# Splitting a resident weight slot two places earlier, and giving one low half in seven to GpSimd

## The reference

```python
x = x + tanh(g_xattn) * xattn(layernorm(x), ctx, mask, Wq, Wk, Wv, Wo, q_norm, k_norm)   # x: 16 x 128 x 1024, 32 heads, 8 KV heads
x = x + tanh(g_ffn) * ffn(layernorm(x), A, B, Wr)
# ffn: scores = x @ Wr.T (64 experts), top 16, softmax -> gates G
#      h = einsum('nd,krd->nkr', x, A);  y = 2 * einsum('nkr,kdr->nd', h * G, B)
```

## Time and profile before

| | us |
|---|---|
| median of 3 executions | 2399.37 (2396.16 to 2401.35) |
| the profiled execution's own time | 2401.17 |
| its span on the core | 2399.4 |
| PE busy | 2289.7 (95%) |
| PEld busy | 1924.3 (80%) |
| DVE busy | 1614.7 (67%) |
| POOL busy | 1313.9 (55%) |
| ACT busy | 1179.2 (49%) |

### The profile page before, as it was taken

The page is one execution under the profiler, slowest core; times in us unless marked ns, Lnnn a source line. Parts: engine busy times, 40 slices in busy tenths (PEclk is TensorE's granted clock), DMA queues, the critical chain, the costliest instruction groups (busy, mean ns, idle before and its releaser), DMA issues.

```text
span 2399.4 us, 35662 instructions
## 1 busy us (share of the span) xinstructions
PE 2289.7 (95%) x11600; PEld 1924.3 (80%) x11600; DVE 1614.7 (67%) x2651; ACT 1179.2 (49%) x3763; POOL 1313.9 (55%) x1811
## 2 busy tenths in 40 slices
PE   5998998999999989999999699999899999999899
PEld 4886887888888878888888588788787787788687
DVE  6557457777777787777777745755756877644755
ACT  4455545666666676666666622422423334333421
POOL 5566567655555575555555344654645655343421
PEclk8999999999999999999999799999999999999999
DMA  4687546757767457742233444545546357324653
GB/s 169 217 229 271 179 158 235 207 165 203 191 167 210 126 175 194 196 135 88 90 95 114 146 159 158 210 167 173 195 159 245 129 204 264 113 81 131 231 174 132
DMA packets 180231, 412.98 MB, mean 172 GB/s; under 512 B 12176, under 2 KB 77968, under 8 KB 164624
## 3 DMA queue, kind: packets, MB, share of 16 engines
q1 hardware_dynamic: 176016, 381.34, 46.6%
q0 software_dynamic: 4032, 29.36, 6.9%
HBM read 293.21 MB, written 176.16 MB: 196 GB/s over the span
## 4 chain that ended last, share of the span: by engine, by line
PE 88%; DVE 3%; issue 3%; POOL 3%; DMA 2%; ACT 1%; SPq 0%; POOLq 0%; ACTq 0%; DVEq 0%
PE bank L706 24%; PE bank L708 24%; PE bank L707 24%; PE bank L764 4%; PE bank L772 2%; PE bank L752 2%; DVE t_lo L1226 1%; PE bank L787 1%; PE bank L789 1%; PE bank L788 1%; DVE s_lo L1226 1%; DMA staged<-in_w_q 1%; PE bank L740 1%; PE bank L723 1%; PE bank L804 1%
## 5 line engine op out<-in xcount | busy, mean ns | idle before, releaser
L706 PE MATMUL bank<-t_hi,s_hi 128*128 128x512 f32 x2688 | 1091.1, 406 | 74.8 <-issue 42.4
L708 PE MATMUL bank<-t_hi,s_lo 128*128 128x512 f32 x2688 | 1059.3, 394 | 0.0
L707 PE MATMUL bank<-t_lo,s_hi 128*128 128x512 f32 x2688 | 1056.9, 393 | 0.0
L706 PEld LDWEIGHTS bank<-t_hi,s_hi 128*128 128x128 f32 x2688 | 510.9, 190 | 182.5 <-issue 82.9
L1226 DVE TENSOR_TENSOR s_lo<-staged,s_hi 128x512 fp32r<-128x512 f32 x672 | 539.9, 848 | 98.9 <-ACT s_hi L954 91.3
L708 PEld LDWEIGHTS bank<-t_hi,s_lo 128*128 128x128 f32 x2688 | 509.3, 189 | 112.1
L707 PEld LDWEIGHTS bank<-t_lo,s_hi 128*128 128x128 f32 x2688 | 511.4, 190 | 91.4
L954 ACT CAST s_hi<-staged 128x512 fp32r<-128x512 f32 x448 | 258.3, 623 | 359.3 <-DMA staged<-heads 190.0
L1646 POOL TENSOR_SCALAR small<-small 128x4 f32<-128x4 f32 (+1 forms) x192 | 65.5, 341 | 417.7 <-ACT small L1039 338.0
L1661 POOL TENSOR_TENSOR staged<-staged 128x512 f32<-128x512 f32 x96 | 136.9, 1426 | 257.3 <-DMA staged<-gated 86.1
L1735 POOL TENSOR_TENSOR sums<-sums,usum 128x512 f32<-128x512 f32 x64 | 97.1, 1538 | 210.5 <-DVE usum L1240 188.7
(11 more groups left out here) (126 smaller groups left out, 2981.1 us busy)
## 6 DMA issues: line engine op xcount, KB each, us to landing
heads<-heads SPq DMA_DIRECT2D x128, 256.0 KB, 3.7
t_raw<-combos SPq DMA_DIRECT2D x28, 1024.0 KB, 8.5
t_raw<-in_sets SPq DMA_DIRECT2D x25, 1024.0 KB, 8.2
staged<-in_w_q SPq DMA_DIRECT2D x32, 768.0 KB, 5.7
staged<-heads SPq DMA_DIRECT2D x32, 768.0 KB, 5.8
sums<-sums SPq DMA_DIRECT2D x18, 1024.0 KB, 7.9
sums<-sums SPq DMA_DIRECT2D x36, 512.0 KB, 4.7
xt<-x_columns SPq DMA_DIRECT2D x8, 1792.0 KB, 7.3
```

The lines of the kernel that those rows point to most:

```text
L706: nc.tensor.matmul(out, s_hi[w][:, cols], high, start=start, stop=False, skip_group_check=True)
L707: nc.tensor.matmul(out, s_hi[w][:, cols], low, start=False, stop=False, skip_group_check=True)
L708: done = nc.tensor.matmul(out, s_lo[w][:, cols], high, start=False, stop=at == 3, skip_group_check=True)
```

## The change

It does four things. (1) The table for the turns at entries 8, 16, 58, 66, 74, 82 and 90 becomes (2, 3, 4, 5, 6, 7, 8): slots 0 to 3 are split two places earlier in the order of ACT and DVE, slots 4 to 6 three places earlier. The turns at 32 and 50 keep their table. (2) From the turn at entry 58 on (set number t of 5 and more), `t_lo[5]` is made by a subtraction on GpSimd instead of DVE; GpSimd has a `fill_t` for it at the end of each place. (3) SP issues the next entry's `staged` ahead of the refill of slot 1 instead of behind it (in the loops with keys and values, output projection and A; not in the query loop). (4) PE's wait on the low half counts on two semaphores instead of one.

```diff
-FILL_POSITIONS = (4, 5, 6, 7, 9, 10, 11)
+FILL_POSITIONS = (2, 3, 4, 5, 6, 7, 8)
...
+    def low_by_pool(self, t, k):
+
+        return t >= 5 and k == 5
+
+    def t_low(self, t, k):
+
+        if self.low_by_pool(t, k):
+            return t - 4
+        return self.t_fill(t, k) - max(t - 5, 0) - (1 if t >= 5 and self.t_order[t].index(k) > 5 else 0)
...
             for j in SEVEN:
-                refill(e, entries[e].ks[j])
                 if j == 1:
                     stage(e + 1, e)
+                refill(e, entries[e].ks[j])
...
-                refill(e, j)
...
                 if j == 1:
                     stage(e + 1, e)
-                    if q and sums_stored(q - 1):
-                        sums_out(q - 1)
+                refill(e, j)
+                if j == 1 and q and sums_stored(q - 1):
+                    sums_out(q - 1)
...
                 if plan.first_of_set[entry.tau] == e:
-                    pe.wait_ge(t_lo_done, plan.t_fill(entry.tau, k))
+                    pe.wait_ge(t_lo_pool if plan.low_by_pool(entry.tau, k) else t_lo_done, plan.t_low(entry.tau, k))
...
             for tau, k in plan.t_due.get(beat, ()):
+                if plan.low_by_pool(tau, k):
+                    continue
                 dve.wait_ge(t_hi_done, plan.t_fill(tau, k))
...
     def _(pool):
+        def fill_t(beat):
+            for tau, k in plan.t_due.get(beat, ()):
+                if plan.low_by_pool(tau, k):
+                    pool.wait_ge(t_hi_done, plan.t_fill(tau, k))
+                    nc.gpsimd.tensor_tensor(t_lo[k][:, :, :], t_raw[k][:, :, :], t_hi[k][:, :, :].bitcast(FP32),
+                                            ALU.subtract).then_inc(t_lo_pool, 1)
```

More of the change, by code:

```diff
@@ L306, in program @@
     t_hi_done, t_lo_done, t0_combo, t0_combo_pool = sem("t_hi_done"), sem("t_lo_done"), sem("t0_combo"), sem("t0_combo_pool")
+    t_lo_pool = sem("t_lo_pool")
     st_in, st12_in = sem("staged_in"), sem("staged12_in")
@@ L1809, in _ @@
                         router_weights()
+                fill_t(plan.beat0[e] + j)
         for e in range(A0, ENTRIES):
```

## The result

The changed kernel takes 2404.27 us (median of 20 executions, 2399.85 to 2411.74) against 2400.23 us (20 executions on the same chip). The ratio is 1.0022, 95% interval 1.0014 to 1.0029: slower by some 4 to 5 us. The forecast was 2392.5 us and 2377 to 2403: the sign was wrong and the time lies just outside the range. The profiled execution's span is 2406.9 us, 7.5 over that of before. That is more than the medians differ by: the profiled execution took 2408.69 us, 4.4 over the median of its kernel, and the one of before 2401.17, 0.9 over.

What follows compares the result with a forecast made beforehand. It took PE, busy 95% of the span, to be held at a turn by DVE's queue, which starts late. Terms 3 x 0 - 4.5 + 1 - 1.0 - 2.4 = -6.9 us gave 2394.3, as median 2392.5 us; range 2377 to 2403.

Steps and rivals of the forecast that it cites:

- The blocking of DVE: At turns with a GpSimd half, DVE stands until GpSimd's long subtraction is through: between 0 and 4.45 us, upper end taken.
- The -4.5 for the turn to 8: Turn to entry 8, no GpSimd half: starts later but ends at 232.9 against 237.43, a win of 4.5 us.
- the +1 for the turn to 16: Turn to entry 16: the phase's last transposes wait behind more resident slots, 1 us lost (from -2 to +4).
- the walk for entry 74: Step-by-step timing of the turn to entry 74: PE stands 4.6 us at the head, product 6 ends at 1879.5, before 1879.51.
- PE does products 0 to 3 without a wait from 1857.0 to 1867.8: In entry 74, behind the 4.6 us wait at its head, PE runs four products without waiting.
- Term: 0.0 us for each of the three turns of the output projection: Turns to entries 58, 66 and 74: slots 4 to 6 early, the evacuation late in their place, no net change.
- rival (b): ACT and DVE stand at a landing, one-piece head gap, clock falls: 2 us at each of six turns, 2407 us, chance 0.18.
- The terms for entries 82 and 90: Turns to entries 82 and 90: wins of 1.0 and 2.4 us, with `s_lo[6]` delayed at both.
- rival (a): The turns open fully, DVE not standing for GpSimd's long subtraction or standing idle: -25 us, time 2374, chance 0.25.
- Point (c): Nothing measurable: at every turn the gap moves from the entry's middle to its head and back; within 4 us of 2399, chance 0.17.
- 0.3 us on the landing of slot 2: Turn to entry 74: SP's new order lands slot 2 0.3 us later and brings `staged` 2.2 us earlier, unused.

Runs made afterwards that it cites:

- the four pieces: The changed kernel with GpSimd's 128x2048 subtraction issued as four of 128x512: 2394.26 us, ratio 0.9969 to the kernel before.
- the memset: The changed kernel with GpSimd's 128x2048 subtraction replaced by a memset of the same tile: 2393.17 us, ratio 0.9962 to the kernel before.
- the sixteen transposes: The changed kernel plus sixteen identity transposes on PE behind product 6 of entries 57, 65 and 73: 2402.22 us, ratio 1.0012 to the kernel before.
- the version that reaches it: The kernel before with table (2, 3, 5, 6, 7, 8, 9), SP's old order, no low half on GpSimd: 2373.42 us, ratio 0.9890.
- the places alone: The kernel before with only the new table (2, 3, 4, 5, 6, 7, 8): 2387.07 us, ratio 0.9953.
- Sixteen 128x128 transposes: The kernel with only the new table, plus identity transposes on PE behind product 6 of entries 57, 65, 73: 2383.04 us, ratio 0.9920 to the kernel before.

## Why the prediction was wrong

**What held.** The blocking of DVE was priced at 4.45 us and measured at 4.69 behind a subtraction of 4.62; the four pieces and the memset show that it is one long instruction that reads SBUF which holds it. This is what the Trainium skill, SBUF — State Buffer, "Who interferes with whom", states of a two-input DVE instruction against a reading GpSimd instruction; the trace agrees (4.69 us), and so does the `s_lo` beside the memset (0.69). The -4.5 for the turn to 8 came out at -4.5, and there the walk had 2.5 us for the slow clock behind the gap (entry 8 took 2.7 us over its 20.88). The same program took 51.3 to 53.8 us there in other executions, so the exact hit is luck. So is the +1 for the turn to 16, which came out at +1.4: the scatter between equal programs is 2.2 us there, and its mechanism was not looked at. In the walk for entry 74, PE was to restart at 1857.0 and did at 1857.23 (1855.69 + 1.54); `third_product` was to end at 1874.1 and did at 1874.80.

**The step that failed** is "PE does products 0 to 3 without a wait from 1857.0 to 1867.8", and with it "Term: 0.0 us for each of the three turns of the output projection". The walk put a gap of 4.6 us in one piece at the head and went on at full clock, although it priced the clock at the turn to 8 and rival (b) says in the same text that it falls behind such a gap. Product 0 took 4.78 us. ACT's evacuation stands behind product 0, `t_hi[5]` behind that evacuation and GpSimd's subtraction behind `t_hi[5]`, so it started at 1865.73 in before's time against 1863.2 in the walk. By then DVE was through with `s_lo` 4 and 5 and `second_product`, and was caught at `s_lo[6]` instead: the order differs from the walk's, and `third_product` ended 0.7 later. Then the second gap, ahead of product 5, was followed by half the clock once more: products 5 and 6 took 4.42 + 2.75 = 7.2 us against the 5.4 of the walk. That is 1.8 of the 2.6 lost at this turn, the later start of product 5 (1873.40 + 1.54 = 1874.94 against 1874.1) the rest. At 66 and 58, product 0 took 5.29 and 4.59 us and the wait ahead of product 5 is there too, but no slow clock behind it.

The memset run shows the same step without the blocking: the walk had 3.4 us to win at each of these turns if DVE did not stand, and the memset kernel wins 1.2, 0.1 and 0.2 us at the turns to 58, 66 and 74. At 74 2.5 of the missing us are the clock behind the head gap.

**The terms for entries 82 and 90** (-1.0 and -2.4) were missed by 3.8 and 5.7 in the profiled execution. There the walk took the half to delay `s_lo[6]`. It caught one of the pair ahead of it, k = 5 in entry 82 and k = 4 in entry 90, and held all that stands behind: DVE in the changed kernel, in entries 82 and 90,

```profile
2041.58 5.73 DVE L1237 TENSOR_TENSOR s_lo<-staged,s_hi 128x512 fp32r<-128x512 f32 x2
...
2244.39 5.67 DVE L1237 TENSOR_TENSOR s_lo<-staged,s_hi 128x512 fp32r<-128x512 f32 x2
```

take 4.4 us more than the 1.28 of such a pair. In entry 82 the router's matmuls then wait 3.0 us for the last `s_lo`. With the half in four pieces entry 82 lasts 26.60 us in place of 31.05, and entry 90 27.98 in place of 31.17.

At the turn to 82 this loss hangs on a few tenths of a us. The changed kernel with the sixteen transposes is the same program there. In its execution DVE was a little ahead when GpSimd's subtraction started, and only `s_lo[6]` stood:

```profile
2041.17 1.29 DVE L1242 TENSOR_TENSOR s_lo<-staged,s_hi 128x512 fp32r<-128x512 f32 x2
...
2044.40 3.08 DVE L1242 TENSOR_TENSOR s_lo<-staged,s_hi 128x512 fp32r<-128x512 f32 x1
```

```profile
2042.10 4.83 POOL L1666 TENSOR_TENSOR t_lo<-t_raw,t_hi 128x2048 fp32r<-128x2048 f32 x1 [12.91 <-ACT t_hi L959]
```

The router did not wait, and the pair took 54.7 us, in place of 59.0 in the changed kernel and 56.3 before: -1.5, near the -1.0 of the walk. So the term for 82 is not shown to be wrong in every execution. That for 90 is: in the same execution entries 89 to 91 took 76.1 us, 0.3 over before. There the half is not the whole of it either. Without the half they took 76.5 us with SP's new order and 72.3 with the old one, against 75.9 before.

**The rivals.** (b) is the sign that came, by half of its own mechanism: ACT stands at slot 1 for 5.32 us and at slot 2 for 0.60, the gap is at the head and the clock falls. But it priced this at 2 us for each of six turns, and left the half's share as in the forecast. Measured with the half taken out, the same gap with its clock is still a win of 5 us over before (0.9979). So in the sum of the parts it is the half, 10 us, that makes a loss of the win. But the half is not what the forecast had wrong: it priced DVE's standing at 3.4 x 3 + 3 + 3 = 16 us. What fell short is the win of the rest. Without the blocking it was to be 25 us, rival (a), and the four pieces and the memset, where that `s_lo` of entry 74 stands for less than a us or not at all, won 7 and 9. (a) would have come at 2374; the version that reaches it, 2373.42, has neither the half nor the three casts ahead of the first `s_hi`. Point (c) describes the walk for entry 74, and what moved that turn off zero was the clock.

**SP's order** is a second term that was sized wrong: the walk charged it 0.3 us on the landing of slot 2 and nothing else, and on the new places it cost 6 to 7 us. It wins where it serves: with the old places `s_hi` was the next cast on ACT when `staged` landed. With three casts ahead of it, the earlier `staged` waits, and what the order costs stays: with the places alone the first `t_hi` of the three starts 7.7 us into entry 57 and the third 17.1 (1504.83 to 1521.89); with SP's order the third starts 17.8 into it (1509.55 to 1527.37). That 0.7 us is read from one turn of each kernel. The pairs at 58, 66 and 74 are 0.9, 0.2 and 0.5 us longer and those at 16 and 82 1.5 and 1.4, of which the one at 16 is within the scatter. Entries 89 to 91 are 4.2 us longer, and 4.6 with the half; this is the largest part, and why it is there was not tried on its own.

## What to carry to other kernels

Price a wait that you gather into one piece with the clock behind it: here the clock behind a gap of 4 to 5 us cost another 1.7 us at the turn where the transposes held it up, and made everything late that stood behind the first product. Before an instruction goes to an engine that can hold up another, look at which short instruction of the other will start inside it: in four pieces the same work cost nothing measurable, in one piece it cost 10 us of 2400, and at one turn a shift of a few tenths of a us decided over 4 of them. And try the parts of a change by themselves: the places and SP's order won 11 and 5.5 us alone, and 5 together.

## What the runs showed of the hardware that was not expected

Four pieces of GpSimd's subtraction took 7.55 us in place of 4.62, with DVE's instruction among them at 2.86; alone such a `t_lo` takes 2.28. Sixteen 128x128 transposes took 1.91 us at the start of a gap and left 2.63, 3.59 and 3.08 us of it idle, where 4.55, 5.23 and 4.48 us had been; they held the granted clock at 1.00 at the first of these turns and halved the slow stretch, from 6.83 to 3.41 us, at the two others.
